# Filing stage of a graph layer on one core: one VectorE product a tile is given to GpSimd

## The reference

```python
def _graph_conv(x, edges, W0, b0, W1, b1):
    src = jnp.concatenate([edges[:, 0], edges[:, 1]])
    dst = jnp.concatenate([edges[:, 1], edges[:, 0]])
    deg = jax.ops.segment_sum(jnp.ones_like(dst, dtype=x.dtype), dst, num_segments=N_NODES)
    deg = jnp.maximum(deg, 1.0)
    agg = jax.ops.segment_sum(x[src], dst, num_segments=N_NODES) / deg[:, None]
    return x @ W0 + b0 + agg @ W1 + b1
...
xn = _layernorm(x, axis=-1)
x = x + _L0_gnn_ref(xn, edge_index_t, ...) + _L0_mix_ref(xn[None], ...)[0]
x = x + _L0_ffn_ref(_layernorm(x, axis=-1)[None], ...)[0]
```

## Time and profile before

| | |
|---|---|
| time, median of 3 runs | 2392.94 us (2387.78 to 2393.01) |
| the profiled execution | 2393.36 us, its span 2391.8 us |
| busy: TensorE / VectorE / ScalarE / GpSimd | 89% / 67% / 50% / 15% of the span |
| filing stage, 38 to 410 us: VectorE busy | 340.30 of 372 us |
| filing stage: TensorE and ScalarE busy | 218.92 and 189.88 of 372 us |
| filing stage: GpSimd busy | 0 us |
| mean granted TensorE clock in the filing stage | 0.64 |

### The profile page before, as it was taken

The page is one execution under the profiler, slowest core; times in us unless marked ns, Lnnn a source line. Parts: engine busy times, 40 slices in busy tenths (PEclk is TensorE's granted clock), DMA queues, the critical chain, the costliest instruction groups (busy, mean ns, idle before and its releaser), DMA issues.

```text
span 2391.8 us, 53412 instructions
## 1 busy us (share of the span) xinstructions
PE 2131.0 (89%) x15340; PEld 1322.6 (55%) x15341; DVE 1611.5 (67%) x4907; ACT 1204.1 (50%) x2432; POOL 352.3 (15%) x427
## 2 busy tenths in 40 slices
PE   2545557999999999999799999999999998699997
PEld 2434445555555555555355554444444443599996
DVE  6999998799999999999444342454444445355554
ACT  2445455455555555555455553444444444466664
POOL 1000000000000000000111110112112112266655
PEclk9665566899999999999899999999999999899998
DMA  3111112622222222222212124555555554655552
GB/s 81 40 34 36 38 32 70 181 110 118 110 117 110 116 114 115 113 117 110 96 51 101 50 70 176 186 207 188 191 204 186 195 200 164 165 95 92 90 92 46
DMA packets 132542, 275.62 MB, mean 115 GB/s; under 512 B 30478, under 2 KB 85951, under 8 KB 130291
## 3 DMA queue, kind: packets, MB, share of 16 engines
q1 hardware_dynamic: 103411, 221.23, 26.5%
q0 software_dynamic: 25216, 44.98, 8.6%
q10 hardware_dynamic: 3840, 8.52, 1.1%
HBM read 137.14 MB, written 132.95 MB: 113 GB/s over the span
## 4 chain that ended last, share of the span: by engine, by line
PE 80%; DVE 8%; issue 4%; DVEq 4%; ACT 1%; POOL 1%; DMA 1%; ACTq 1%; SPq 0%; POOLq 0%
PE bank L2127 44%; PE bank L2118 6%; PE bank L2348 6%; PE bank L2333 6%; PE bank L2280 5%; PE bank L2268 5%; DVE big L1034 2%; PE bank L2283 2%; DVE big L1048 1%; DVEq L1063 1%; PE bank L2315 1%; DVEq L1031 1%; DVEq L1044 1%; PE bank L2135 1%; PE bank L1996 1%
## 5 line engine op out<-in xcount | busy, mean ns | idle before, releaser
L2127 PE MATMUL bank<-RW,big 128*128 128x512 f16 (+1 forms) x4900 | 1180.1, 380 | 4.9 <-DMA big<-a_dram 4.7
L2127 PEld LDWEIGHTS bank<-RW,big 128*128 128x128 f16 x4900 | 443.8, 98 | 401.6 <-issue 9.1
L1784 ACT ACTIVATE big<-bank 128x512 f16<-128x512 f32 (+1 forms) x640 | 371.7, 581 | 317.5 <-PE bank L2118 317.5
L1181 DVE TENSOR_TENSOR big<-iotaB,keys 128x512 f16<-128x512 f16 x1300 | 451.7, 416 | 7.9 <-issue 7.8
L2118 PEld LDWEIGHTS bank<-big 128*128 128x128 f16 x2560 | 190.8, 98 | 111.5 <-issue 1.2
L2118 PE MATMUL bank<-big 128*128 128x128 f16 x2560 | 247.2, 219 | 0.7 <-issue 0.7
L899 POOL DMA_INDIRECT out_dram<-big x112 | 178.4, 1593 | 136.2 <-ACT big L1941 102.3
L842 POOL DMA_DIRECT2D big<-in_L_ffn_W_dram x8 | 6.4, 804 | 1145.0 <-DVE R L1240 1142.1
L1932 ACT ACTIVATE big<-bank,b1A,iscA 128x256 f32<-128x256 f32 x224 | 114.3, 560 | 99.2 <-PE bank L2333 93.9
L2333 PE MATMUL bank<-big,RW 128*128 128x256 f16 x1344 | 157.9, 275 | 3.7 <-ACT big L1921 3.7
L2348 PE MATMUL bank<-RW,big 128*128 (+1 forms) x1344 | 155.9, 273 | 0.0
(11 more groups left out here) (396 smaller groups left out, 2971.5 us busy)
## 6 DMA issues: line engine op xcount, KB each, us to landing
big<-a_dram SPq DMA_DIRECT2D x49, 832.0 KB, 6.0
big<-a_dram SPq DMA_DIRECT2D x49, 768.0 KB, 4.5
a_dram<-big SPq DMA_DIRECT2D x49, 640.0 KB, 3.0
a_dram<-big SPq DMA_DIRECT2D x49, 512.0 KB, 2.6
a_dram<-big SPq DMA_DIRECT2D x49, 448.0 KB, 2.5
big<-rows_dram SPq DMA_DIRECT2D x56, 265.0 KB
big<-in_x_dram SPq DMA_DIRECT2D x96, 128.0 KB, 2.1
big<-in_L_ffn_W_dram POOLq DMA_DIRECT2D x16, 512.0 KB, 4.6
```

What stands on the lines that cost most here:

```text
L1181: last = v.tensor_tensor(out[q].rearrange("p b (m k) -> p b m k", k=2), inturn(iotaB[:, :], QB, P // 2), twice(kd[:, q * QB:(q + 1) * QB, ...
L1784: a.activation(Ab[q][:, 0:n], banks[BB(q)][:, 0:n], ACT.Copy).then_inc(s_ab, 1)
L2127: last = mm(bank[:, :], blk(q, c), src, start=(u == 0), stop=(u == T))
```

## The change

The product `V` of a tile leaves VectorE's program and becomes one GpSimd instruction with the same operands. GpSimd waits for the one-hots of the tile (`s_oh`) and, from the fourth tile on, for a free buffer (`s_filed`). VectorE now waits with `s_val` before it overwrites a buffer of `OH`, and SyncE waits for the last `V` before it blanks the words.

```diff
@@ sync @@
             sp.wait_ge(s_xl, T)
+            sp.wait_ge(s_val, T)
             blank(0, at_pairs // D)
@@ gpsimd @@
             nc.gpsimd.memset(pwait[:, :], 0.0)
+
+            def values(t):
+
+                pool.wait_ge(s_oh, t + 1)
+                if t >= 3:
+                    pool.wait_ge(s_filed, t - 2)
+                nc.gpsimd.tensor_tensor(V[t % 3].bitcast(F32).rearrange("p (c u) -> p c u", c=CAP),
+                                        OH[t % 2].rearrange("p (c u) -> p c u", c=CAP),
+                                        endsF[:, t * CAP:(t + 1) * CAP].rearrange("p (c o) -> p c o", o=1)
+                                        .to_broadcast([P, CAP, U]), ALU.mult).then_inc(s_val, 1)
+
+            for t in range(T):
+                values(t)
+
             pool.wait_ge(s_flag, 2)
@@ vector, onehots @@
                 if t >= 2:
                     dve.wait_ge(s_before, t - 1)
+                    dve.wait_ge(s_val, t - 1)
                 v.tensor_tensor(oh, inturn(iotaU[:, :], CAP, U // 2), twice(key2[:, sl, :], CAP, U // 2),
                                 ALU.is_equal).then_inc(s_oh, 1)
                 dve.drain()
-                if t >= 3:
-                    dve.wait_ge(s_filed, t - 2)
-                v.tensor_tensor(V[t % 3].bitcast(F32).rearrange("p (c u) -> p c u", c=CAP),
-                                OH[par].rearrange("p (c u) -> p c u", c=CAP), deep(endsF[:, sl], [P, CAP, U]),
-                                ALU.mult).then_inc(s_val, 1)
```

## The result

The change made the kernel slower: 2419.46 us median (2419.11 to 2421.42, 4 runs) against 2390.41 for the kernel before (4 runs). The ratio is 1.0124, 95% interval 1.0111 to 1.0137, so +29 us. The profiled execution has a span of 2417.5 us.

A forecast was written before the change was run, and what follows sets the result against it. VectorE's queue was taken to bound the filing stage. Each tile loses 2.13 - 0.08 = 2.05 us and gains 1.11, net +0.94; 48 tiles give +45 us, so 2438 us, range 2392 to 2470.

The forecast's parts named there:

- VectorE's queue binds the stage: Filing stage: it lasts as long as VectorE's instructions and small gaps, VectorE being busy 340.30 of 372 us.
- The removal gives 1.11 us a tile: VectorE's queue in the filing stage: taking V out returns 1.11 us for each of 48 products, 53.3 us.
- The new waits and the three buffers cost nothing: Filing stage: VectorE's and SyncE's new waits cost nothing and three V buffers suffice, GpSimd being hidden up to about 6 us.
- GpSimd's reads and VectorE's two-input instructions exclude each other: SBUF access: a reading GpSimd instruction and a two-input VectorE instruction shut each other out for whole instructions, whichever starts first.
- the two pairs: Start of the trace: L755 (0.70 us) beside L952, and L947 (0.53 us) beside a select, each later one held.
- VectorE's L1042 is first, then GpSimd, at the same price as the other way round: Behind a tile's one-hots: L1042 (0.67 us) runs first, V then holds L1046; GpSimd first would cost the same.
- the gap: VectorE's existing 0.08 us gap between L1042 and L1046, taken to lie inside the hold and subtracted from it.
- The hold is 2.13 us: V's block on VectorE per tile: 0.89 plus 1.16 ns an element for 1000 elements, 2.05 us, and 0.08 for the start.
- The first rival's floor: No exclusion, so ScalarE's loop limits a filing-stage tile to 5.81 or 5.03 us; 2340 to 2362 us; chance 13%.
- My likelier end, 2362: Whole time without exclusion, -31 us, with about a quarter of the filing stage at TensorE's upper level.

The follow-up runs named there:

- e1: Changed kernel with V computed on neither engine, its semaphores kept; output wrong, only the filing stage read: 322.6 us, 43.9 less than in the kernel before.
- e11: e1 with the slow fallback for missing edges switched off, to time the whole program; output wrong; 2348.84 us, ratio 0.9827 to the kernel before.
- e2: Changed kernel with GpSimd writing all of V by memset and reading nothing; output wrong, only the filing stage read: 320.6 us.
- e3: Changed kernel with GpSimd copying the one-hots to V (one float16 input) instead of multiplying; output wrong; VectorE's product held for 0.84 us.
- e6: Changed kernel with GpSimd's V waiting for VectorE's folding addition, so that it starts with the one-input sum; 2388.69 us, ratio 0.9985 to the kernel before.
- e5: Changed kernel with a one-number write and a drain ahead of each GpSimd product, so that it starts later; 2409.7 us in one run.
- e9: e8 with VectorE multiplying 6 of the 20 groups and GpSimd the other 14; 2361.25 us, ratio 0.9878 to the kernel before.
- e8: Changed kernel without the folding addition, the sum taking all 1000 elements and GpSimd's V starting with it; 2366.29 us, ratio 0.9889 to the kernel before.

## Why the prediction was right, and where its sizes were off

- **VectorE's queue binds the stage.** Right. The stage follows VectorE tile by tile, and the change of its length, +28.7 us, is that of the median, +29.
- **The removal gives 1.11 us a tile.** Right by the tile. Without any V the stage gains 43.9 and the program 41 us of the 53 (e1, e11). Most of the difference is ScalarE's square root, which then binds in part of the tiles: inside the stage VectorE's waits for it are 11.3 - 4.5 = 6.8 us in e1, against 4.0 - 3.2 = 0.8 before. In the change itself the only such wait is the one ahead of the first tile:

```profile
DVE rstd L1073 <- ACT sums L1692: 4.5, 1, 4.5
```

- **The new waits and the three buffers cost nothing.** Right within 0.03 us a tile; e1 has all of them.
- **GpSimd's reads and VectorE's two-input instructions exclude each other.** Right, and shown from several sides: a write doesn't hold VectorE (e2), one input does (e3), the one-input sum is free (e6), and who starts first keeps the other out (the change and e5). One of the two pairs that the prediction read this from is no example of it, though: the cast L947 has one input and was held all the same, 0.53 us for 52 columns. So one input alone doesn't make a VectorE instruction free; why the cast was held, no run tests.
- **VectorE's L1042 is first, then GpSimd, at the same price as the other way round.** This step failed in both halves. GpSimd's row started 0.01 us ahead of VectorE's and L1053 was held, not the addition. And the order has a price: with VectorE first a tile is 0.20 us shorter (e5), some 0.14 us for the part of V that passes beside VectorE's product and 0.08 for the gap. What the change paid is the dearer of the two.
- **The hold is 2.13 us.** Mis-sized: it measured 1.70. The term was 0.89 ns for the float16 and 1.16 ns for the float32 stream, taken from the selects; the runs show 0.84 ns for the float16 stream (e3) and 0.86 for the float32 one, by the difference. A float32 select, which reads and writes, was no measure of what a second input costs. With 1.70, and no gap of 0.08 to hide in, the sum is 48 x (1.70 - 1.11 + 0.03) = +30 us, where 29 were measured and 45 forecast. The hold alone takes 48 x 0.43 = 21 us off the forecast; the missing gap puts 4 back and the 0.03 one more. That the errors partly cancel is luck. From the "GPSIMD Engine Reference" of the Trainium skill (section "Performance versus the Vector engine"), with its 4497 ns for 2048 float32 elements, the estimate for V was 2.20 us; the row is 1.85 us, and of that 1.70 hold. The measurement decides.
- **The first rival's floor.** It gave 2340 to 2362 for a V that costs nothing; e11 has 2349. My likelier end, 2362, took the share of TensorE's upper level as fixed, and it rose (a mean granted clock of 0.78 in e11 against 0.64).

## What to carry to other kernels

An idle GpSimd isn't a free helper for VectorE: each element that it reads costs a two-input VectorE instruction about 0.85 ns, so a product with two inputs, 1.11 us on VectorE, came back as 1.70. Before such a move, list VectorE's instructions in the order in which they run and look for one that GpSimd's reading doesn't disturb. Here that was the sum, shown at two lengths (e6 to e9), and a semaphore can put the reading beside it. For other one-input instructions nothing here shows it, and the cast L947 speaks against it: test the one at hand. It can even pay to make VectorE's one-input stretch longer (a full sum instead of a fold and a sum, at equal length) to give GpSimd its room: that turned +29 us into -26 (e8) and -28 (e9).

## What the runs showed of the hardware that I had not expected

- The time of a held instruction stands in its own row (L1053 at 2.375 us instead of 0.67) and not in the idle time ahead of it.
- GpSimd's elementwise instructions hold a two-input VectorE instruction for about 0.85 ns per element and input, with nearly no fixed part: 0.84 us for 1000 x 1 input, 0.86 for 500 x 2, 1.70 for 1000 x 2. The hold is some 0.15 us shorter than GpSimd's row (1.85, and 1.02 twice).
- When the one-hots ended, GpSimd, which a semaphore releases, started ahead of VectorE's own next instruction in all 48 tiles, by 0.01 us as the rows show it, and with this order a tile was 0.2 us longer than with the other (e5).
